# First cross-attention: quantised rows as whole numbers in bf16 with the scales applied to the products, and the first loads in another order

## The chip, the cores and the metric

The kernel runs on one core of a Trainium2 chip. The metric is the time of one execution on the device, in microseconds (us), taken as the median over several executions. The engines are named as in the profile: PE (TensorE, matrix products) with PEld (its weight loads), DVE (VectorE), ACT (ScalarE), POOL (GpSimd) and SP (the engine that issues the DMAs).

## The reference

Six stages run over x, 16 sequences of 32 tokens of 256 features (512 rows): cross-attention, differential attention, an fp8 feed-forward, a second cross-attention, latent attention and a second fp8 feed-forward. The change touches the first. It is preceded by a layer norm of x and followed by the residual sum, and attends to a context of 512 tokens of 256 features for each sequence, with 16 heads of 16 features:

```
s    = max(|row|) / 127                          # one scale per row
qdq(a) = clip(round(a / s), -127, 127) * s
q    = qdq(y) @ qdq(wq).T + bq                   # y = layernorm(x)
k, v = ctx @ wk.T + bk, ctx @ wv.T + bv
o    = softmax(q k.T / 4) v
x    = x + qdq(o) @ qdq(wp).T + bp
```

qdq takes one scale per token for an activation and one per output channel for a weight. Since both scales are constant along the summed features, they can be taken out of the product: (whole numbers of y) @ (whole numbers of wq).T, times the scale of the token, times the scale of the channel.

## The kernel before

The program is written out for each engine in its own order; engines meet at semaphores. The first cross-attention is `xattn` with L0 true, and has two parts.

**The opening** runs up to the first scores. SP issues the loads in one order: x, the key weights, the value weights, the context of batch 0, the key bias, the identity matrix, then wq, wp, the biases and the head mask (`load_rest`), then further contexts (`load_later`). PE first waits for the identity (in `build`), then for three loads of weights and bias (`s_kv_in`) and for the context. It computes keys and values in "units", four to a batch: units 0 and 1 of a batch are the two halves of the keys (L355), units 2 and 3 the values (L361). A unit fills one of two PSUM banks, which ACT (later DVE too) empties into SBUF (L585, L587); a bank must be emptied before the unit after next. ACT takes units 0 to 15 here. Between units, PE turns wq (L509), turns the normed rows of x (L152), forms the queries (L517) and turns wp. DVE prepares these operands: `norm_stats`, then `qdq_rows` on wq, on y and on wp, with copies of what PE turned (L864, L873). ACT and DVE each finish one half of the queries (L690, L870), and POOL spreads them by head (`separate`).

**The batch loop** (`batch_rows_pe`, `batch_rows_act`, `batch_rows_dve`) runs over 16 batches. PE computes four scores (L375), turns four sets of probabilities (`turn`, L400), multiplies them with the values (`values`, L422), and works three or four units ahead for later batches. DVE takes the maxima (L717) and copies half of the turned probabilities (L722); ACT takes the exponentials (L605) and copies the other half (L617). Groups 2 and 3 of a batch are turned and multiplied in the next batch.

Four batches make one tile of 128 output rows. In batches 6, 10 and 14 the loop also finishes a tile: in the batch before, DVE normalises, adds the bias and runs `qdq_rows` on it (`rows_ready`); PE turns it (`turn_out`, L449), ACT copies it (`copy_out_cols`, L634), PE multiplies it with wp (`out_rows`, L458) and DVE adds the product to x (`residual`, L770). The fourth tile is done after the loop. From batch 6 to batch 13, DVE ends each batch with a centring of attention weights for the next stage (L960 to L965).

Of the kernel before, what the change touches and what calls it, by code (L numbers as in the profile page):

```python
# [14 lines left out]
P = 128  # L15
# [164 lines left out]
def qdq_rows(nc, ch, rows, n, q):  # L180
# [8 lines left out]
    for i in range(n):  # L189
        ch.mark(nc.vector.tensor_scalar(rows[:, i, :], rows[:, i, :], -127.0, q.s[:, i:i + 1], ALU.max, ALU.mult))  # L190
    ch.join()


def xattn(nc, e, take, sem, L0, d):
# [3 lines left out]
    s_w, s_kv_in = sem(f"{nm}_weights"), sem(f"{nm}_wkv_in")  # L198
    ctx_in = [sem(f"{nm}_ctx_in{i}") for i in range(CB)]
# [28 lines left out]
    wqT, wpT = (take([P, NC, D]), take([P, NC, D])) if L0 else (wq, wp)  # L228
# [4 lines left out]
    orow, orT = take([P, NT, D]), take([P, NC, P])  # L233
    rc = take([P, 4, H])
    oc = take([P, G, P])
    if L0:
        q = Named(m=take([P, NT]), s=take([P, NT]), r=take([P, NT]))
# [12 lines left out]
    U, S, T, O = (B[0], B[1]), (B[2], B[3], B[4], B[5]), (B[4], B[5]), (B[6], B[7])  # L250
    TURNB, OUTB, YB = O[1], O[0], O[1] if L0 else O[0]
# [89 lines left out]
    def unit_pe(pe, u):  # L341
# [6 lines left out]
        if i == 0:  # L348
            if b == 0:
                pe.wait_ge(s_kv_in, 48)  # L350
            pe.wait_ge(ctx_in[b % CB], 16 * (b // CB + 1))
# [5 lines left out]
        else:  # L357
            for kk in range(2):
# [80 lines left out]
    def turn_out(pe, t):  # L439
# [8 lines left out]
        for c in range(NC):  # L448
            last = nc.tensor.transpose(OUTB[:, c * P:(c + 1) * P], orow[:, t, c * P:(c + 1) * P], e.ident)  # L449
# [55 lines left out]
    def turn_weight(pe, i):  # L505
        pe.wait_ge(s_wq, i + 1)
        for c in range(NC):
            for o in range(NC):
                last = nc.tensor.transpose(B[2 + i][:, c * D + o * P:c * D + (o + 1) * P],  # L509
                                           (wq, wp)[i][:, o, c * P:(c + 1) * P], e.ident)  # L510
        last.then_inc(s_wT, 1)

    def queries(pe):
        pe.wait_ge(e.s_yT_out, f.all)
        for c2 in range(NC):
            for c in range(NC):
                last = nc.tensor.matmul(B[4 + c2], wqT[:, c, c2 * P:(c2 + 1) * P], e.yT[:, c, :],  # L517
# [3 lines left out]
    def pe(pe):  # L521
        if L0:
            for u in range(8):
                unit_pe(pe, u)
            turn_weight(pe, 0)
            for u in range(8, 12):
                unit_pe(pe, u)
            for k in range(2):
                norm_turn(nc, pe, e, f, k, O[k])
            pe.wait_ge(s_wT_out, 1)  # L530
# [4 lines left out]
            pe.wait_ge(s_wT_out, 2)  # L535
# [107 lines left out]
    def batch_rows_act(act, b):  # L643

        copy_out_cols(act, tile_at(b, OUT))
        if b:
            copy_pT_act(act, b - 1, 2)
        exp_rows(act, b, 0), exp_rows(act, b, 1)
# [27 lines left out]
    def act(act):  # L676
        act.wait_ge(s_kv_in, 48)
        if L0:
            for u in range(12):
                unit_act(act, u)  # L680
            for k in range(2):
                norm_cols(nc, act, e, f, k, O[k], e.yT)
# [50 lines left out]
    def rows_ready(v, t):  # L733
# [22 lines left out]
        if L0:  # L756
            e.ch.link(nc.vector.tensor_tensor(orow[:, t, :], orow[:, t, :], bv, ALU.add))
            qdq_rows(nc, e.ch, orow[:, t:t + 1, :], 1, q)
# [4 lines left out]
    def residual(v, t):  # L763
# [74 lines left out]
    def before_dve(v):  # L838
# [8 lines left out]
        nc.vector.tensor_scalar(bs, bq, DH ** -0.5, None, ALU.mult).then_inc(s_small, 1)  # L847

    def dve(v, done):
        if L0:  # L850
# [5 lines left out]
            qdq_rows(nc, e.ch, wq, NC, q)  # L856
            v.sem_inc(s_wq, 1)
            for k in range(2):
                norm_rows(nc, v, e, f, k, e.s_norm)
            v.wait_ge(e.s_norm, NT)  # L860
            qdq_rows(nc, e.ch, e.Y, NT, q)
# [3 lines left out]
            qdq_rows(nc, e.ch, wp, NC, q)  # L865
            v.sem_inc(s_wq, 1)
        else:
            before_dve(v)
        v.wait_ge(s_qT, 2)
        nc.vector.tensor_scalar(qT[:, 1, :], B[5], bq[:, 1:2], DH ** -0.5, ALU.add, ALU.mult).then_inc(s_qT_out, 1)  # L870
        if L0:
            v.wait_ge(s_wT, 2)
            nc.vector.tensor_copy(wpT.rearrange("p c n -> p (c n)"), B[3]).then_inc(s_wT_out, 1)  # L873
# [999 lines left out]

def build(nc, d, out, stages=6):
    with ExitStack() as ctx:
# [8 lines left out]
        neghalf = sb("neg_half", [P, 2 * NT])  # L1884
# [10 lines left out]
        s_const, s_x, s_half, s_chain = sem("constants"), sem("x_in"), sem("neg_half_ready"), sem("dve_chain")  # L1895
        done = [sem(f"phase_done{i}") for i in range(stages)]
# [8 lines left out]
        def _(sp):  # L1905
            sp.dma_start(e.X, d.x.rearrange("(t p) d -> p t d", p=P)).then_inc(s_x, 16)
            phases[X0].load_early(sp, 1)
# [49 lines left out]
        def _(pe):  # L1957
            pe.wait_ge(s_const, 16)
# [80 lines left out]
```

## Time and profile before

| | us |
|---|---|
| median of 3 executions | 745.14 |
| lowest and highest | 739.39, 746.81 |
| profiled execution | 744.93 |
| its span, first to last instruction | 743.1 |
| opening: start to first scores | 45.5 |
| batch loop and last tile: first scores to the last tile's residual sum | 192.3 |

The span is what the rows below are placed in; a start is counted from its beginning. "Busy" is time in which an engine has an instruction under way, and an idle time in brackets names what ended it. The product of two fp32 operands appears in the trace as two passes for each matmul of the program, and a turn (transpose) of an fp32 tile as one.

### The profile page before, as it was taken

To read this page: it belongs to the slowest core of one execution; us is meant where nothing else is said; L and a number is where in the kernel's file an instruction comes from. 1 tells how busy PE (TensorE), PEld (TensorE's weight loads), DVE (VectorE), ACT (ScalarE), POOL (GpSimd) and SP (SyncE) were. 2 spreads that over 40 slices of the span, in tenths; PEclk is the share of its full clock that TensorE was granted. 3 is DMA by queue.
4 is the path that set the end of the run, shared out by engine and by line. 5 is a ranking of instruction groups with operands and counts; after the bars stand their busy time and mean duration, and the time that the engine had idled before them with its cause. 6 is when DMAs were issued, how large, how long until landed. Compare 5 with 4: busy or idle time off the path is not lost.

```text
span 743.1 us, 21667 instructions
## 1 busy us (share of the span) xinstructions
PE 672.0 (90%) x9593; PEld 443.3 (60%) x9594; DVE 424.0 (57%) x979; ACT 278.1 (37%) x503; POOL 76.3 (10%) x138
## 2 busy tenths in 40 slices
PE   4999999999997999999988999999989978899744
PEld 2656566666654677777765566776657754366512
DVE  4324446567475655555533945547757844465477
ACT  1334434344442333333335625444434443121123
POOL 1020000001001011111112412010101001000000
PEclk9999999999999999999999999999999999999967
DMA  5242101114101701110004301111850000000000
GB/s 187 86 147 46 47 30 30 51 38 146 56 2 39 248 30 32 34 36 17 2 1 151 134 28 59 59 31 50 225 169 3 4 2 0 3 4 4 3 1 29
DMA packets 39357, 42.02 MB, mean 57 GB/s; under 512 B 13216, under 2 KB 29856, under 8 KB 39008
## 3 DMA queue, kind: packets, MB, share of 16 engines
q1 hardware_dynamic: 39264, 40.63, 17.6%
q8 instruction: 76, 1.25, 0.7%
q14 instruction: 17, 0.14, 0.1%
HBM read 40.10 MB, written 0.52 MB: 55 GB/s over the span
## 4 chain that ended last, share of the span: by engine, by line
PE 76%; DVE 15%; issue 3%; ACT 3%; POOL 1%; DMA 1%; SPq 0%; DVEq 0%; ACTq 0%; POOLq 0%
PE psum L355 14%; PE psum L361 13%; PE psum L1023 6%; PE psum L422 4%; PE psum L375 4%; PE psum L400 4%; PE psum L389 4%; PE psum L1070 4%; PE psum L1029 3%; PE psum L1678 2%; PE psum L1054 2%; PE psum L1697 2%; DVE arena L1347 1%; PE psum L1043 1%; PE psum L1654 1%
## 5 line engine op out<-in xcount | busy, mean ns | idle before, releaser
L355 PE MATMUL psum<-arena 128*128 128x512 f32 x256 | 125.1, 616 | 11.6 <-DMA ident<-in_ident 9.2
L361 PE MATMUL psum<-arena 128*128 128x256 f32 x512 | 124.4, 389 | 0.4 <-ACT arena L585 0.4
L361 PEld LDWEIGHTS psum<-arena 128*128 128x128 f32 x512 | 94.6, 192 | 24.0 <-issue 9.4
L355 PEld LDWEIGHTS psum<-arena 128*128 128x128 f32 x256 | 45.8, 194 | 57.3 <-issue 42.3
L611 ACT ACTIVATE arena<-arena 128x512 f32<-128x512 f32 x64 | 48.6, 806 | 77.8 <-DVE arena L730 77.8
L422 PEld LDWEIGHTS psum<-arena 128*17 128x17 f32 x4096 | 38.9, 96 | 32.0 <-issue 26.0
L730 DVE TENSOR_SCALAR arena<-psum 128x512 f32<-128x512 f32 x64 | 41.2, 685 | 28.5 <-PE psum L389 27.0
L605 ACT ACTIVATE arena<-psum,arena 128x512 f32<-128x512 f32 x64 | 42.5, 688 | 37.9 <-DVE arena L717 37.8
L717 DVE TENSOR_REDUCE arena<-psum 128x1 f32<-128x512 f32 x64 | 42.4, 685 | 22.7 <-PE psum L375 22.6
L1023 PE MATMUL psum<-y_cols,arena 128*128 128x512 f32 x112 | 52.2, 599 | 0.0
L422 PE MATMUL psum<-arena 128*17 128x32 f32 x4096 | 45.0, 195 | 7.5 <-ACT arena L611 3.4
L303 POOL TENSOR_TENSOR arena<-arena,head_mask 128x128 f32<-128x128 f32 x64 | 24.9, 413 | 217.8 <-PE psum L375 123.3
L1118 ACT ACTIVATE arena<-psum 128x512 f32<-128x512 f32 x48 | 28.2, 597 | 49.8 <-PE psum L1023 31.8
L389 PE MATMUL psum<-arena 64*128 64x128 f32 x512 | 38.1, 288 | 2.4 <-POOL arena L303 1.7
L585 ACT ACTIVATE arena<-psum,arena 128x512 f32<-128x512 f32 x41 | 27.9, 683 | 32.0 <-PE psum L355 31.9
L389 PEld LDWEIGHTS psum<-arena 64*128 64x128 f32 x512 | 31.8, 190 | 12.4 <-issue 8.0
L722 DVE COPY arena<-psum 128x512 f32<-128x512 f32 x32 | 22.1, 690 | 27.5 <-PE psum L400 27.0
L587 ACT ACTIVATE arena<-psum 128x512 f32<-128x512 f32 x41 | 24.3, 594 | 35.1 <-PE psum L361 35.1
L400 PEld LDWEIGHTS psum<-ident,arena 128*128 128x128 f32 x256 | 28.7, 141 | 14.1 <-issue 12.3
L375 PE MATMUL psum<-arena 64*128 64x512 f32 x128 | 36.1, 641 | 0.0
L400 PE MATMUL psum<-ident,arena 128*128 128x128 f32 x256 | 34.1, 276 | 0.8 <-ACT arena L605 0.8
L617 ACT ACTIVATE arena<-psum 128x512 f32<-128x512 f32 x32 | 19.1, 597 | 39.3 <-PE psum L400 39.0
(229 smaller groups left out, 979.9 us busy)
## 6 DMA issues: line engine op xcount, KB each, us to landing
arena<-in_ctxT SPq DMA_DIRECT2D x32, 512.0 KB, 3.7
arena<-in_L_attn_Wv SPq DMA_DIRECT2D x1, 2048.0 KB, 8.3
arena<-in_L_attn_Wq SPq DMA_DIRECT2D x8, 256.0 KB, 2.9
arena<-in_L_attn_Wk SPq DMA_DIRECT2D x8, 256.0 KB, 3.3
arena<-in_L_attn_Wo SPq DMA_DIRECT2D x1, 2048.0 KB, 11.5
arena<-in_L_ffn_w_gating SPq DMA_DIRECT2D x1, 2048.0 KB, 7.8
arena<-in_L_attn_wo SPq DMA_DIRECT2D x1, 2048.0 KB, 10.7
arena<-in_wq_upT SPq DMA_DIRECT2D x1, 1536.0 KB, 8.5
```

The lines of the kernel that those rows point to most:

```text
L355: last = nc.tensor.matmul(bank, wkv[:, c, i * P:(i + 1) * P], x[:, c, :], start=(c == 0), stop=(c == NC - 1))
L361: last = nc.tensor.matmul(bank[:, kk * D:(kk + 1) * D], x[:, c, k * P:(k + 1) * P], wkv[:, c, D:2 * D], start=(c == 0), stop=(c == NC - 1))
L375: nc.tensor.matmul(S[r], qbd[b % 2][a, h, :, :].rearrange("p j q -> p (j q)"), kT[home(b)][a, h, :], start=True, stop=True).then_inc(s_sco ...
L389: ins = nc.tensor.matmul(S[2 * kp + r][:, (2 * kk + h) * P:(2 * kk + h + 1) * P], kT[home(b)][a, h, k * P:(k + 1) * P], qbd[b % 2][a, h, : ...
L400: last = nc.tensor.transpose(T[g % 2][:, k * P:(k + 1) * P], pr[g % 2][:, k * P:(k + 1) * P], e.ident)
L422: last = nc.tensor.matmul(O[b % 2][j * SQ:j * SQ + VW, g * SQ:(g + 1) * SQ], va[home(b)][:, k, HG * g + j, :], probs[:, j * SQ:(j + 1) * S ...
L605: nc.scalar.activation(pr[g % 2], S[g % 2], ACT.Exp, bias=nmx[:, g:g + 1]).then_inc(s_exp, 1)
L611: nc.scalar.activation(pTk[b % 2][k], clip[k // 2][:, k % 2, :], ACT.Exp, bias=mb[:, b, k:k + 1], scale=m01[:, b, k:k + 1]).then_inc(s_exp, 1)
L717: nc.vector.tensor_reduce(nmx[:, g:g + 1], S[g % 2], AX.X, ALU.max, negate=True).then_inc(s_mx, 1)
L730: nc.vector.tensor_scalar(dst, S[i].rearrange("p (a n) -> p a n", n=P), 50.0, -50.0, ALU.min, ALU.max)\
L1023: last = nc.tensor.matmul(bank, w[:, c, f], e.yT[:, c, :], start=(c == 0), stop=(c == NC - 1))
L1070: ins = nc.tensor.matmul(ACC[t // 2][:, (t % 2) * D:(t % 2 + 1) * D], oT[h % 2][:, t, :], wo[:, h, :], start=(h == 0 and t % 2 == 0), stop ...
```

## The change

**Whole numbers.** `qdq_rows` becomes `whole_rows`: the last step, which clipped and multiplied each row by its scale, only clips and writes the whole numbers as bf16 (-127 to 127 are exact there). The turned copies (`wqT`, `wpT`, `yT8`, `orT`) are bf16, so the products for the queries and for the output rows have bf16 operands, and the turns multiply by a bf16 identity, which DVE makes (L904 of the changed kernel).

**Scales.** The token scales are needed along the columns. PE spreads them over a bank with four 128x128 products (`token_scales`), DVE copies that bank to SBUF and applies both scales to each half of the queries; ACT adds the bias to both halves. The channel scales of wp go the same way (`channel_scales`, `swp`), and `residual` first applies both scales, then adds to x.

**Loads and start.** The order is now: key weights, context of batch 0, value weights, key bias, x, identity, and the rest as before. The key weights have a semaphore of their own, so units 0 and 1 wait for it and for the context only; the identity is waited for where it is first used. Before its first unit PE runs three matmuls on a constant (`first_busy`), ACT one small activation.

**Order in a tile's batch.** `turn_out` comes after the two turns of the batch before, `out_rows` after its values; ACT's copies are exchanged likewise.

```diff
-def qdq_rows(nc, ch, rows, n, q):
+def whole_rows(nc, ch, rows, n, q, whole):
...
     ch.link(nc.vector.tensor_scalar(rows, rows, ROUND, 127.0, ALU.subtract, ALU.min))
-    for i in range(n):
-        ch.mark(nc.vector.tensor_scalar(rows[:, i, :], rows[:, i, :], -127.0, q.s[:, i:i + 1], ALU.max, ALU.mult))
-    ch.join()
+    ch.link(nc.vector.tensor_scalar(whole, rows, -127.0, None, ALU.max))
...
-        for dst, src in ((wkv[:, :, 0:D], cols(d.wkT)), (wkv[:, :, D:2 * D], cols(d.wvT))):
-            sp.dma_start(dst, src).then_inc(s_kv_in, 16)
+        sp.dma_start(wkv[:, :, 0:D], cols(d.wkT)).then_inc(s_wk, 16)
         load_ctx(sp, 0)
+        sp.dma_start(wkv[:, :, D:2 * D], cols(d.wvT)).then_inc(s_kv_in, 16)
...
-                pe.wait_ge(s_kv_in, 48)
+                pe.wait_ge(s_wk, 16)
...
+            if u == 2:
+                pe.wait_ge(s_kv_in, 32)
...
+        if b == 0 and g == 0:
+            pe.wait_ge(s_wT_out, 3)
...
-            last = nc.tensor.transpose(OUTB[:, c * P:(c + 1) * P], orow[:, t, c * P:(c + 1) * P], e.ident)
+            cols = slice(c * P, (c + 1) * P)
+            if L0:
+                last = nc.tensor.matmul(OUTB[:, cols], whole[:, t, cols], identb, start=True, stop=True)
...
         scores_rows(pe, b, 0)
-        turn_out(pe, tile_at(b, OUT))
         if b:
             turn(pe, b - 1, 2), turn(pe, b - 1, 3)
+        turn_out(pe, tile_at(b, OUT))
         unit_pe(pe, slot(b, 0))
-        out_rows(pe, tile_at(b, TAKE))
         if b:
             values(pe, b - 1, 2), values(pe, b - 1, 3)
+        out_rows(pe, tile_at(b, TAKE))
...
+    def token_scales(pe):
+
+        pe.wait_ge(s_wT_out, 1)
+        for t in range(NT):
+            nc.tensor.matmul(TOKENS[:, t * P:(t + 1) * P], qx.s[:, t:t + 1].to_broadcast([P, P]), e.ident, start=True, stop=True)
+
+    def channel_scales(pe):
+
+        pe.wait_ge(s_wT_out, 2)
+        pe.wait_ge(s_qT_out, 2)
+        for c in range(NC):
+            last = nc.tensor.matmul(CHANNELS[:, c * P:(c + 1) * P], qp.s[:, c:c + 1].to_broadcast([P, P]), e.ident,
+                                    start=True, stop=True)
...
+            for c in range(NC):
+                act.wait_ge(s_small, c + 1)
+                nc.scalar.activation(qT[:, c, :], qT[:, c, :], ACT.Identity, bias=bs[:, c:c + 1]).then_inc(s_qT_out, 1)
...
+            e.ch.link(nc.vector.scalar_tensor_tensor(out=orow[:, t, :], in0=OUTB[:, D:2 * D], scalar=qx.s[:, 0:1], in1=swp,
+                                                     op0=ALU.mult, op1=ALU.mult))
             v.wait_ge(s_xb, t + 1)
-            nc.vector.tensor_tensor(e.X[:, t, :], OUTB[:, D:2 * D], e.X[:, t, :], ALU.add).then_inc(s_res, 1)
+            nc.vector.tensor_tensor(e.X[:, t, :], orow[:, t, :], e.X[:, t, :], ALU.add).then_inc(s_res, 1)
...
+            v.wait_ge(s_qT, 1)
+            e.ch.link(nc.vector.tensor_copy(pr[0], TOKENS))
+            for c in range(NC):
+                v.wait_ge(s_qT, c + 1)
+                nc.vector.scalar_tensor_tensor(out=qT[:, c, :], in0=B[4 + c], scalar=swq[:, c:c + 1], in1=pr[0],
+                                               op0=ALU.mult, op1=ALU.mult).then_inc(s_small, 1)
+            v.wait_ge(s_wT, 2)
+            nc.vector.tensor_copy(wpT.rearrange("p c n -> p (c n)"), B[3]).then_inc(s_wT_out, 1)
+            v.wait_ge(s_wT, 3)
+            nc.vector.tensor_copy(swp, CHANNELS).then_inc(s_wT_out, 1)
...
+def first_busy(nc, e, bank, n):
+
+    for _ in range(n):
+        nc.tensor.matmul(bank, e.neghalf[:, 0:1].to_broadcast([P, P]), e.neghalf[:, 0:1].to_broadcast([P, 512]),
+                         start=True, stop=True)
...
-            sp.dma_start(e.X, d.x.rearrange("(t p) d -> p t d", p=P)).then_inc(s_x, 16)
             phases[X0].load_early(sp, 1)
+            sp.dma_start(e.X, d.x.rearrange("(t p) d -> p t d", p=P)).then_inc(s_x, 16)
...
-            pe.wait_ge(s_const, 16)
+            pe.wait_ge(s_half, 1)
+            first_busy(nc, e, e.B[5], 3)
...
+            act.wait_ge(s_half, 1)
+            nc.scalar.activation(warm, e.neghalf2, ACT.Identity)
```

Three places of PE's order follow. At the start, before (in brackets the semaphores waited for):

```order
L355 MATMUL psum<-arena 128x512 [waits x0_ctx_in0,x0_wkv_in,constants]
L355 MATMUL psum<-arena 128x512 x3
L361 MATMUL psum<-arena 128x256 [waits x0_unit_out0]
L361 MATMUL psum<-arena 128x256 x3
L361 MATMUL psum<-arena 128x256 [waits x0_unit_out1]
L361 MATMUL psum<-arena 128x256 x3
L355 MATMUL psum<-arena 128x512 [waits x0_ctx_in1,x0_unit_out0]
L355 MATMUL psum<-arena 128x512
```

and with the change, where L359 and L367 are the units' lines L355 and L361:

```order
L1934 MATMUL psum<-neg_half 128x512 [waits neg_half_ready]
L1934 MATMUL psum<-neg_half 128x512 x2
L359 MATMUL psum<-arena 128x512 [waits x0_ctx_in0,x0_wk_in]
L359 MATMUL psum<-arena 128x512 x3
L367 MATMUL psum<-arena 128x256 [waits x0_wkv_in,x0_unit_out0]
L367 MATMUL psum<-arena 128x256 x3
L367 MATMUL psum<-arena 128x256 [waits x0_unit_out1]
L367 MATMUL psum<-arena 128x256 x3
L359 MATMUL psum<-arena 128x512 [waits x0_ctx_in1,x0_unit_out0]
```

The identity ("constants") no longer stands ahead of unit 0, three matmuls on the constant do, and the value weights and key bias are waited for at unit 2.

From the turns of the normed rows to the next unit, before:

```order
L152 MATMUL psum<-ident,y_rows 128x128 [waits y_rows]
L152 MATMUL psum<-ident,y_rows 128x128 x3
L152 MATMUL psum<-ident,y_rows 128x128 [waits y_rows]
L152 MATMUL psum<-ident,y_rows 128x128 x3
L517 MATMUL psum<-y_cols,arena 128x512 [waits y_cols_out,x0_wT_out]
L517 MATMUL psum<-y_cols,arena 128x512 x3
L509 MATMUL psum<-ident,arena 128x128 [waits x0_wqdq]
L509 MATMUL psum<-ident,arena 128x128 x3
```

and with the change:

```order
L531 MATMUL psum<-arena 128x128 [waits y_rows]
L531 MATMUL psum<-arena 128x128 x3
L531 MATMUL psum<-arena 128x128 [waits y_rows]
L531 MATMUL psum<-arena 128x128 x3
L538 MATMUL psum<-ident,arena 128x128 [waits x0_wT_out]
L538 MATMUL psum<-ident,arena 128x128 x3
L553 MATMUL psum<-arena 128x512 [waits y_cols_out]
L553 MATMUL psum<-arena 128x512 x3
L521 MATMUL psum<-arena 128x128 [waits x0_wqdq]
L521 MATMUL psum<-arena 128x128 x3
L359 MATMUL psum<-arena 128x512 [waits x0_ctx_in0,x0_unit_out0]
```

L531 are the bf16 turns, L538 the token scales, L553 the queries, L521 the turn of wp. Four 128x128 products have come in ahead of the queries.

In batch 6, before (L375 scores, L449 `turn_out`, L400 turns, L361 a unit, L458 `out_rows`, L422 values):

```order
L375 MATMUL psum<-arena 128x512 x2
L449 MATMUL psum<-ident,arena 128x128 x2
L400 MATMUL psum<-ident,arena 128x128 x8
L361 MATMUL psum<-arena 128x256 x4
L458 MATMUL psum<-arena 128x256 x2
L422 MATMUL psum<-arena 17x32 x32
L355 MATMUL psum<-arena 128x512 x2
```

and with the change (L381, L459, L408, L367, L470, L430 in their place):

```order
L381 MATMUL psum<-arena 128x512 x2
L408 MATMUL psum<-ident,arena 128x128 x8
L459 MATMUL psum<-arena 128x128 x2
L367 MATMUL psum<-arena 128x256 x4
L430 MATMUL psum<-arena 17x32 x32
L470 MATMUL psum<-arena 128x256 x2
L359 MATMUL psum<-arena 128x512 x2
```

`turn_out` has moved behind eight turns, and `out_rows` behind the 32 products of two groups' values.

## Rows read from the trace of the kernel before

**Rows 1.** Page, busy time by engine: us, share, instructions.
```profile
PE 672.0 (90%) x9593; PEld 443.3 (60%) x9594; DVE 424.0 (57%) x979; ACT 278.1 (37%) x503; POOL 76.3 (10%) x138
```

**Rows 2.** Stretches, 10 to 15 us: PE, PEld, DVE, ACT, POOL busy, PEclk, DMA, GB/s.
```profile
10.00:15.00 5.00, 4.60 (x9) 1.76 (x8) 2.95 (x10) 2.20 (x3) 1.38 (x2) 1.00 0.54 194
```

**Rows 3.** Timeline of the DMA issues: start, us, line, transfer.
```profile
1.24 0.49 SPq L268 DMA_DIRECT2D arena<-in_L_wkT  x1
...
2.29 0.47 SPq L263 DMA_DIRECT2D arena<-in_ctxT  x1
2.80 0.47 SPq L270 DMA_DIRECT2D arena<-in_L_xattn_bkv  x1
...
6.94 18.90 SPq L263 DMA_DIRECT2D arena<-in_ctxT  x4
```

**Rows 4.** DMA issues: KB, us to landing; contexts of batches 0 and 1 last.
```profile
arena<-in_L_wkT SPq DMA_DIRECT2D x1, 256.0 KB, 4.4
...
arena<-in_L_xattn_bkv SPq DMA_DIRECT2D x1, 1.0 KB, 6.1
...
arena<-in_ctxT SPq DMA_DIRECT2D x1, 512.0 KB, 6.4
...
arena<-in_ctxT SPq DMA_DIRECT2D x1, 512.0 KB, 5.8
```

**Rows 5.** Chain of waits, 0 to 62 us: start, us, engine, line.
```profile
9.16 3.56 PE psum L355 x4
...
12.79 1.28 ACT L585
...
14.82 3.72 PE psum L361 x16
18.55 3.44 PE psum L355 x8
...
32.80 0.60 ACT arena L587
...
34.52 3.67 PE psum L517 x8
...
45.53 1.06 PE psum L375 x4
```

**Rows 6.** Timeline of VectorE, 0 to 62 us.
```profile
11.73 0.17 DVE L847 TENSOR_SCALAR arena<-arena 128x2 f32<-128x2 f32 x1 [4.11 <-DMA head_mask<-in_headmask]
...
19.83 1.14 DVE L190 TENSOR_SCALAR y_rows<-y_rows,arena 128x256 f32<-128x256 f32 x4
```

**Rows 7.** Timeline of TensorE in the first feed-forward: 8-bit operands.
```profile
401.41 1.89 PE L1287 MATMUL psum<-arena 128*128 128x512 fp8e4 x8 [0.97 <-ACT arena L160]
```

**Rows 8.** Chain of waits in batch 6, then TensorE's waits, 95 to 230 us.
```profile
113.93 0.87 PE psum L400 x8
...
116.53 0.87 PE psum L458 x4
...
PE psum L449 <- DVEq L759: 1.7, 3, 0.6
```

**Rows 9.** Timeline of VectorE in batch 6, of both in 10, of VectorE in 14.
```profile
120.89 0.69 DVE L722 COPY arena<-psum 128x512 f32<-128x512 f32 x1 [3.03 <-PE psum L400]
...
161.63 0.44 PE L449 MATMUL psum<-ident,arena 128*128 128x128 f32 x2 [0.59 <-DVEq L759]
...
164.47 0.68 DVE L722 COPY arena<-psum 128x512 f32<-128x512 f32 x1
...
165.46 0.73 PE L422 MATMUL psum<-arena 128*17 128x32 f32 x64
...
212.04 0.68 DVE L722 COPY arena<-psum 128x512 f32<-128x512 f32 x1
```

**Rows 10.** Chain of waits at the end of the stage.
```profile
236.26 1.15 PE psum L458 x4
237.43 0.43 DVE x_rows L770
```

More of the change, by code:

```diff
@@ L227, in xattn @@
     wq, wp = take([P, NC, D]), take([P, NC, D])
-    wqT, wpT = (take([P, NC, D]), take([P, NC, D])) if L0 else (wq, wp)
+    wqT, wpT = (take([P, NC, D], BF16), take([P, NC, D], BF16)) if L0 else (wq, wp)
     bq, bs = take([P, NC]), take([P, NC])
@@ L232, in xattn @@
     qT = take([P, NC, ROWS])
-    orow, orT = take([P, NT, D]), take([P, NC, P])
+    orow, orT = take([P, NT, D]), take([P, NC, P], BF16 if L0 else F32)
     rc = take([P, 4, H])
@@ L236, in xattn @@
     if L0:
-        q = Named(m=take([P, NT]), s=take([P, NT]), r=take([P, NT]))
+        qx, qq, qp = (Named(m=take([P, NT]), s=take([P, NT]), r=take([P, NT])) for _ in range(3))
+        wq8 = take([P, NC, D], BF16)
+        wp8 = wq.rearrange("p c n -> p (c n)").bitcast(BF16)[:, 0:NC * D].rearrange("p (c n) -> p c n", c=NC)
+        whole, yT8 = take([P, NT, D], BF16), take([P, NC, ROWS], BF16)
+        identb, swq, swp = take([P, P], BF16), take([P, NC]), take([P, D])
         nmx = take([P, HG])
@@ L508, in turn_weight, with turn_tokens @@
             for o in range(NC):
-                last = nc.tensor.transpose(B[2 + i][:, c * D + o * P:c * D + (o + 1) * P],
-                                           (wq, wp)[i][:, o, c * P:(c + 1) * P], e.ident)
+                last = nc.tensor.matmul(B[2 + i][:, c * D + o * P:c * D + (o + 1) * P],
+                                        (wq8, wp8)[i][:, o, c * P:(c + 1) * P], identb, start=True, stop=True)
+        last.then_inc(s_wT, 1)
+    def turn_tokens(pe, k):
+        ts = f.groups[k]
+        pe.wait_ge(e.s_y, f.y + ts[-1] + 1)
+        for c in range(NC):
+            for j, t in enumerate(ts):
+                a = (c * len(ts) + j) * P
+                last = nc.tensor.matmul(O[k][:, a:a + P], whole[:, t, c * P:(c + 1) * P], identb, start=True, stop=True)
+        last.then_inc(e.s_yT, 1)
+    def token_scales(pe):
[8 more added lines that the diff above has]
+                                    start=True, stop=True)
         last.then_inc(s_wT, 1)
@@ L516, in queries @@
             for c in range(NC):
-                last = nc.tensor.matmul(B[4 + c2], wqT[:, c, c2 * P:(c2 + 1) * P], e.yT[:, c, :],
+                last = nc.tensor.matmul(B[4 + c2], wqT[:, c, c2 * P:(c2 + 1) * P], (yT8 if L0 else e.yT)[:, c, :],
                                         start=(c == 0), stop=(c == NC - 1))
@@ L534, in pe @@
                 unit_pe(pe, u)
-            pe.wait_ge(s_wT_out, 2)
+            channel_scales(pe)
         else:
@@ L687, in act @@
                     unit_act(act, u)
-        act.wait_ge(s_qT, 1)
-        act.wait_ge(s_small, 1)
-        nc.scalar.activation(qT[:, 0, :], B[4], ACT.Identity, bias=bs[:, 0:1], scale=DH ** -0.5).then_inc(s_qT_out, 1)
+        if L0:
+            for c in range(NC):
+                act.wait_ge(s_small, c + 1)
+                nc.scalar.activation(qT[:, c, :], qT[:, c, :], ACT.Identity, bias=bs[:, c:c + 1]).then_inc(s_qT_out, 1)
+        else:
+            act.wait_ge(s_qT, 1)
+            act.wait_ge(s_small, 1)
+            nc.scalar.activation(qT[:, 0, :], B[4], ACT.Identity, bias=bs[:, 0:1], scale=DH ** -0.5).then_inc(s_qT_out, 1)
         for u in range(12 if L0 else FIRST - 2, FIRST):
@@ L757, in rows_ready @@
             e.ch.link(nc.vector.tensor_tensor(orow[:, t, :], orow[:, t, :], bv, ALU.add))
-            qdq_rows(nc, e.ch, orow[:, t:t + 1, :], 1, q)
+            whole_rows(nc, e.ch, orow[:, t:t + 1, :], 1, qx, whole[:, t:t + 1, :])
             v.sem_inc(s_or, 1)
@@ L846, in before_dve @@
             e.ch.join()
[L847 removed]
+        if L0:
+            e.ch.link(nc.vector.tensor_scalar(bs, bq, DH ** -0.5, None, ALU.mult))
+        else:
+            nc.vector.tensor_scalar(bs, bq, DH ** -0.5, None, ALU.mult).then_inc(s_small, 1)
     def dve(v, done):
@@ L860, in dve @@
             v.wait_ge(e.s_norm, NT)
-            qdq_rows(nc, e.ch, e.Y, NT, q)
+            whole_rows(nc, e.ch, e.Y, NT, qx, whole)
             v.sem_inc(e.s_y, NT)
@@ L1883, in build @@
         arena = sb("arena", [P, WORDS])
-        neghalf = sb("neg_half", [P, 2 * NT])
+        neghalf, warm = sb("neg_half", [P, 2 * NT]), sb("act_warm", [P, 2 * NT])[:, :]
         e = Named(
```

33 lines of the change are left out of this document (20 added, 13 removed).

## The prediction

> **What bounds the kernel now.** I read the page first: PE is busy 90% of the span, DVE 57%, ACT 37% [rows 1]. Then the chain of waits and the timeline of the first 62 us, where nearly all edits lie, and then the chain in the batches that finish a tile. In the opening the chain is PE almost without a break from 9.16 us to the first scores at 45.53 [rows 5]. Ahead of 9.16 it is a transfer, the identity matrix. Four things on it are not steady PE work. The start is one. The first four passes take 3.56 us where eight later ones take 3.44, so 0.89 each against 0.43: that is the rate of the 1.2 GHz level, and the later ones that of 2.4. PE had done nothing before them. The granted clock of the stretch reads 1.00 [rows 2, 5], so this slow start has to be read from the passes themselves. ACT's table load at 12.79 delays the first emptied bank, so that unit 2 starts at 14.82. And between the last unit and the queries PE waits for ACT: from 32.80 to 34.52. In the batch loop PE is the chain too, except before the turn of a finished tile [rows 8].
>
> **The start.** Today PE waits for the last of five loads. With the change it needs the key weights and the context of batch 0, now the first two issues. Today the first two (x and key weights, 512 + 256 KB) had landed at 1.24 + 4.4 = 5.64 us [rows 3, 4]; the new pair has the same bytes, so 5.6 is the early bound. The context itself took 6.4 us from its issue; from the second slot, 1.24, that is 7.6, the late bound. It then shared the engines with 1,024 KB ahead of it, now with 256, so I take 6.0, near the early one. Gain 9.16 - 6.0 = **3.2** (1.6 to 3.5).
>
> **The warm-up.** Three fp32 matmuls of 512 columns are six passes. They can start at about 0.9, some 0.1 after the first DMA is issued, since they wait only for a constant that POOL writes first. Four at 0.89 and two at 0.43 give 4.4 us, so they end at 5.3, before the context lands; all six at 0.89 would end at 6.2, a delay of 0.2. The first eight real passes then take 3.44 instead of 3.56 + 1.72: **1.8** less. The table load now runs at about 1 us beside the loads, and unit 2 starts when unit 1 ends: **0.4** less (14.82 - 14.44). The key bias must be there when unit 0 ends, at 7.7: it landed 6.1 after its issue [rows 4], which from its new slot at 2.29 gives 8.4, so bank 0 is empty at about 9.1, still before unit 2 is due at 9.4. I cost it at nothing, or 0.5 if it comes as late as before.
>
> The Trainium skill ("TensorE: Matmul & The Clock Gate", Part 1) says that the point at which the array turns fast varies from run to run of the same kernel, so a fixed number of warm-up matmuls need not reach it. No run here can show that yet; it is the second rival.
>
> **What could now come first.** Everything on PE up to the queries moves 5.4 us earlier, and its partners must keep up. The context of batch 1, issued at 6.94 with 5.8 to landing, is there at 12.7; unit 4 is due at 6.0 + 6.9 = 12.9. That is only just hidden (0 to 0.5 if not). x now lands at about 8.7, as the context did, instead of 4.9. DVE's statistics then take 2.7 us and end near 11.4, and DVE was waiting until 11.73 for the head mask anyway [rows 6]: nothing. The whole numbers of y, finished at about 21 [rows 6], are needed at 27: 6 us of cover.
>
> **Queries.** The gap from the last unit to the queries is ACT's, one bank of 0.60 and two copies, and stays at 1.7 us. The bf16 turns and the four 128x128 scale products (some 1.0 us, eight passes of 0.11 to 0.13) lie inside it. The queries were eight passes in 3.67 us. bf16 has no row of this kind in this stage; the nearest is the fp8 product, eight matmuls of 512 columns in 1.89 [rows 7]: one pass a matmul, some 0.21 each when the first one's start-up is taken off, so 0.11 for 256 columns. Four passes instead of eight twice as long: 0.85 against 3.44, **2.6** less. At the other bound, weight loading that stops bf16 from being faster than one fp32 pass, 1.7 instead of 0.85, it is 1.7 less. Both turns of weights become bf16, four passes that took 0.44 each time: **0.4** less together. `channel_scales` adds two products, four passes, ahead of the scores: **0.5** more.
>
> DVE then has a longer chain than before: copy, two scalings, with ACT's two bias adds behind (five operations of 0.6 to 0.7, two overlapping), and ACT cannot empty units 12 and 13 before the second of them. Queries half one done at 29.1, copy to 29.8, scalings to 30.5 and 31.2, ACT done at 32.0, unit 12 emptied at 32.7; unit 14 is due at 33.1. Hidden by units 12 and 13, with 0.4 to spare; without that cover it would cost its excess one to one. The sum to the first scores: 3.2 + 1.8 + 0.4 + 2.6 + 0.4 - 0.5 = **7.9**.
>
> **The batch loop.** Each of three tiles loses 0.65 in `out_rows` (four passes in 0.87, now two of 0.11) and 0.3 in its turn (0.44 with its start-up [rows 9], now inside the stream). The wait before the turn, 1.7 in three, goes because eight turns (0.87) stand ahead of it [rows 8]. That would be 1.5 a tile. But DVE is late next. In batch 10 its centring work comes after the tile's rows, and its copy for group 3 ends at 165.15, when PE reached the values at 165.46 only because the wait and the slower `out_rows` stood before them [rows 9]. With the change PE is free at 161.63 - 0.59 = 161.04 and reaches group 3 after the turns (0.87), the tile's turn (0.12), a unit (1.72) and group 2 (0.33), at 164.1, and stands 1.0 there. So batch 10 gains 0.5. In batch 14 the copy ends at 212.72, PE gets there at 212.3, gain 1.05. Together 1.5 + 0.5 + 1.05 = **3.1** (0 to 4.6). The extra DVE operation in `residual` (0.43) is covered: DVE idles 3.03 ahead of its next copy [rows 9].
>
> **The last tile** is a chain with no cover: `out_rows` (1.15 there) 0.65 and its turn 0.1 shorter, DVE's two operations in place of one 0.43 more [rows 10]: **0.3** less. Its wait for DVE does not go, since the turn hangs on DVE's rows themselves.
>
> **The sum.** 7.9 + 3.1 + 0.3 = 11.3. Later stages are not touched and follow on the stage's end. The profiled execution took 744.93 (span 743.1); 744.93 - 11.3 = 733.6. It lies 0.2 below the median 745.14, so I predict **733.6** as median too. The three executions spread over 7 us without any row that explains it.
>
> **Rivals.**
> 1. *The forecast*, 0.57: 727.5 to 737, from the late bounds (2.5 less gain) and from the larger loop gain with an early context.
> 2. *The warm-up does not carry*, 0.13: the array is slow again or still when the context lands, and four passes cost 1.8 more, with the transfer late by 1.0: 736.5. For it: PE idles between 5.3 and the landing. Against: that is under 1 us, and PE keeps its speed over the 1.7 us gap before the queries. The rule of the Trainium skill given above stands behind it.
> 3. *The loop gives nothing*, 0.15: PE's gain in a tile's batch turns into a wait for DVE or for ACT's exponentials, as batch 10 half shows. 733.6 + 3.1 = 736.7.
> 4. *bf16 operands do not save the passes*, 0.05: the trace would show as many passes as before. Without 2.6 + 0.4 + 3 x 0.75 + 0.75 = 6.0: 739.6.
> 5. *DVE becomes the bound of the tile batches*, 0.10, slower at its end: `out_rows` now comes later, DVE stands at `residual` for it, with the copy of group 1 and two maxima queued behind, and PE needs those for its next turns. DVE today idles 3 us ahead of that copy; if PE waited out a tile's rows (3.2) and the two residual operations (0.9) in each of three batches, 12.3 us, against 8.2 gained outside the loop, it would be 749. It decides from 2.7 us a tile. Against it: PE has a unit of 1.7 and eight turns between.
>
> **Numbers.** Less than 1% either way (7.4 us, about what a measurement of this kernel can tell) counts as the same. Faster by over 1%, below 737.7: nearly all of cases 1 to 3, less what the spread of the runs takes: 0.77. Same: 0.18, from case 4, the mild end of 5 and drift of the runs. Slower: 0.05, the end of 5. The range 727 to 739.5 leaves out most of case 5 and the tails.
>
> **What would show it.** Right: the first unit near 6.0 with all passes at 0.43; no table load between units; the first scores near 37.6; four query passes in about 1; eight turns, then the tile's turn without a wait; a wait for DVE's copy ahead of group 3's values in batches 10 and 14, near 1.0 and 0.4. Wrong: a first unit after 7.6, slow passes in it, a gap before unit 4 or unit 14, or PE waits in the tile batches above 1.5 us.

## The result, and the profile after

| us | before | changed |
|---|---|---|
| median (4 executions each) | 743.77 | 733.80 |
| lowest and highest | 739.39, 746.81 | 730.49, 735.92 |
| profiled execution, and its span | 744.93, 743.1 | 730.49, 728.7 |

The ratio of the times is 0.9864, 95% interval 0.9827 to 0.99: 10 us faster. A second measurement beside the experiments gave 731.36 against 746.45, ratio 0.9819 (0.9787 to 0.985).

PE is busier by share, for nearly the same work in less time; it remains the bound (the columns are those of [rows 1]):

```profile
PE 669.4 (92%) x9600; PEld 440.9 (61%) x9600; DVE 426.7 (59%) x983; ACT 278.2 (38%) x505; POOL 76.1 (10%) x138
```

The first loads, as KB and us to landing, answer to [rows 4]. The last row is the context of batch 0:

```profile
x_rows<-in_x SPq DMA_DIRECT2D x1, 512.0 KB, 5.9
arena<-in_L_wkT SPq DMA_DIRECT2D x1, 256.0 KB, 2.8
...
arena<-in_L_xattn_bkv SPq DMA_DIRECT2D x1, 1.0 KB, 4.6
...
arena<-in_ctxT SPq DMA_DIRECT2D x1, 512.0 KB, 3.8
```

It had landed at 1.24 + 3.8 = 5.04 us, and the key bias at 2.25 + 4.6 = 6.9. PE's timeline at the start of the changed kernel:

```profile
0.89 4.66 PE L1934 MATMUL psum<-neg_half 128*128 128x512 f32 x6 [0.89 <-POOL neg_half L2014]
5.38 3.60 PE L359 MATMUL psum<-arena 128*128 128x512 f32 x8
...
12.82 3.68 PE L359 MATMUL psum<-arena 128*128 128x512 f32 x8 [0.38 <-DMA arena<-in_ctxT]
```

The six passes of the constant (two for each of the three matmuls) took 4.66 us, the first unit followed them directly (no idle time stands behind the row), all eight of its passes ran at the fast rate, and unit 4 waited 0.38 for its context. The chain of waits through the queries answers to [rows 5]:

```profile
27.15 0.60 ACT arena L624
...
28.78 1.04 PE psum L553 x4
29.82 0.23 PE psum L521 x4
...
37.00 0.44 PE psum L545 x4
37.44 1.06 PE psum L381 x4
```

The gap from the last unit to the queries is 28.78 - 27.15 = 1.63 (1.72 before). The queries take 1.04 instead of 3.67, the turn of wp 0.23, the channel scales 0.44, and the first scores stand at 37.44 instead of 45.53: **8.1 us** earlier.

In the loop, the chain in batch 6, then PE's timeline in batch 10 and the sum of one kind of wait, answer to [rows 8, 9]:

```profile
104.80 1.02 PE psum L408 x8
105.82 0.11 PE psum L459 x2
...
107.71 0.66 PE psum L430 x50
108.38 0.33 PE psum L470 x2
...
155.58 0.43 PE L430 MATMUL psum<-arena 128*17 128x32 f32 x32 [0.83 <-DVE arena L764]
...
PE psum L430 <- DVE arena L764: 1.3, 3, 0.8
```

The tile's turn costs 0.11 behind the eight turns and waits for nothing; `out_rows` costs 0.33 with its start-up. In its place PE now waits for DVE's copy of group 3: 0.83 in batch 10 and 0.18 in batch 14 (the rest of the 1.3 is in the last batch and was there before).

The end of the last tile answers to [rows 10]:

```profile
224.88 0.41 PE psum L470 x2
...
225.31 0.50 DVE arena L811
225.83 0.44 DVE x_rows L814
```

The tile is multiplied in 0.41 instead of 1.15, and DVE applies the scales (L811) in 0.50 before it adds.

From the first scores to the last tile's sum it is now 226.27 - 37.44 = 188.8 instead of 192.3: **3.5 us** less. The stage therefore ends 11.6 earlier, and the rest of the span went from 505.3 to 502.4 although nothing in it was changed. The last section comes back to that.

### The profile page after: what moved, and what is told of

It is laid out like the page before. It is cut to its first block, busy times and chain, and to the rows that moved or that the text cites. A ratio compares the mean times of both kernels' runs of the same rounds, so it can differ in the third digit from the quotient of the medians.

```text
span 728.7 us, 21690 instructions
## 1 busy us (share of the span) xinstructions
PE 669.4 (92%) x9600; PEld 440.9 (61%) x9600; DVE 426.7 (59%) x983; ACT 278.2 (38%) x505; POOL 76.1 (10%) x138
## 4 chain that ended last, share of the span: by engine, by line
PE 77%; DVE 15%; issue 3%; ACT 2%; POOL 1%; SPq 1%; DMA 1%; DVEq 0%; POOLq 0%; ACTq 0%
PE psum L359 13%; PE psum L367 13%; PE psum L1080 7%; PE psum L430 5%; PE psum L381 4%; PE psum L395 4%; PE psum L408 4%; PE psum L1127 4%; PE psum L1086 4%; PE psum L1735 2%; PE psum L1111 2%; PE psum L1754 2%; DVE arena L1404 1%; PE psum L1100 1%; PE psum L1711 1%
## 5 line engine op out<-in xcount | busy, mean ns | idle before, releaser
L359 PE MATMUL psum<-arena 128*128 128x512 f32 x256 | 122.5, 605 | 2.8 <-DVEq L172 2.0
L367 PE MATMUL psum<-arena 128*128 128x256 f32 x512 | 124.3, 388 | 0.0
L367 PEld LDWEIGHTS psum<-arena 128*128 128x128 f32 x512 | 94.6, 192 | 23.3 <-issue 9.7
L359 PEld LDWEIGHTS psum<-arena 128*128 128x128 f32 x256 | 44.7, 189 | 47.7 <-issue 41.9
L430 PEld LDWEIGHTS psum<-arena 128*17 128x17 f32 x4096 | 39.5, 97 | 32.0 <-issue 24.7
L430 PE MATMUL psum<-arena 128*17 128x32 f32 x4096 | 46.1, 197 | 6.2 <-ACT arena L648 3.5
L408 PEld LDWEIGHTS psum<-ident,arena 128*128 128x128 f32 x256 | 28.6, 141 | 16.4 <-issue 14.6
L381 PE MATMUL psum<-arena 64*128 64x512 f32 x128 | 36.1, 641 | 0.0
L408 PE MATMUL psum<-ident,arena 128*128 128x128 f32 x256 | 34.2, 276 | 0.8 <-ACT arena L642 0.8
## 6 DMA issues: line engine op xcount, KB each, us to landing
arena<-in_L_attn_Wo SPq DMA_DIRECT2D x1, 2048.0 KB, 11.7
```

The costliest lines, as they stand in the source:

```text
L359: last = nc.tensor.matmul(bank, wkv[:, c, i * P:(i + 1) * P], x[:, c, :], start=(c == 0), stop=(c == NC - 1))
L367: last = nc.tensor.matmul(bank[:, kk * D:(kk + 1) * D], x[:, c, k * P:(k + 1) * P], wkv[:, c, D:2 * D], start=(c == 0), stop=(c == NC - 1))
L381: nc.tensor.matmul(S[r], qbd[b % 2][a, h, :, :].rearrange("p j q -> p (j q)"), kT[home(b)][a, h, :], start=True, stop=True).then_inc(s_sco ...
L408: last = nc.tensor.transpose(T[g % 2][:, k * P:(k + 1) * P], pr[g % 2][:, k * P:(k + 1) * P], e.ident)
L430: last = nc.tensor.matmul(O[b % 2][j * SQ:j * SQ + VW, g * SQ:(g + 1) * SQ], va[home(b)][:, k, HG * g + j, :], probs[:, j * SQ:(j + 1) * S ...
```

## The experiments

"Opening" is the start of the first scores by PE's timeline (37.37 in the changed kernel, 45.46 before), "loop" the time from there to the end of the last tile's sum (188.9 and 192.4), "rest" what is left of the span. These three are read from one profiled execution of each kernel. "(one)" is the time of a single execution. The rows e1 to e4, e5 to e8 and f1 to f4 are three groups on different chips, so a time is best compared within its group: beside them the kernel before took 744.9, 747.2 (one) and 746.5.

| kernel | first unit | opening | loop | rest | time, us |
|---|---|---|---|---|---|
| before | 9.16 | 45.46 | 192.4 | 505.3 | 743.8 |
| changed | 5.38 | 37.37 | 188.9 | 502.4 | 733.8 |
| e1, start only | 6.17 | 40.18 | 192.9 | 501.1 | 737.0 |
| e2, numbers only | 9.81 | 43.90 | 189.0 | 506.7 | 739.3 |
| e3, no matmuls ahead | 5.31 | 39.41 | 189.2 | 509.7 | 740.0 (one) |
| e4, old order | 6.02 | 37.39 | 189.6 | 502.8 | 731.6 (one) |
| e5, two matmuls ahead | 5.29 | 36.97 | 190.0 | 504.7 | 733.5 (one) |
| e6, context 1 early | 6.17 | 38.00 | 188.9 | 504.2 | 732.9 (one) |
| e7, two more copies | 6.17 | 39.08 | 188.9 | 503.6 | 733.3 (one) |
| e8, centring moved | 6.17 | 37.70 | 190.2 | 503.1 | 732.8 (one) |
| f1, changed again | 5.40 | 37.16 | 188.9 | 502.9 | 731.4 |
| f2, combined | 5.33 | 36.78 | 188.7 | 506.4 | 731.5 |
| f3, paced loads | 6.13 | 37.51 | 188.9 | 503.9 | 732.0 |
| f4, no activation ahead | 5.17 | 37.83 | 188.9 | 501.5 | 730.1 (one) |

### Two halves of the change: e1 and e2

e1 adds to the kernel before:

```diff
+        sp.dma_start(wkv[:, :, 0:D], cols(d.wkT)).then_inc(s_wk, 16)
         load_ctx(sp, 0)
+        sp.dma_start(wkv[:, :, D:2 * D], cols(d.wvT)).then_inc(s_kv_in, 16)
...
+            first_busy(nc, e, e.B[5], 3)
...
+            nc.scalar.activation(warm, e.neghalf2, ACT.Identity)
```

> The kernel before with the start of the change alone (order of the first loads, separate waits, three matmuls and one activation ahead); numbers, scales and the order of the tile batches as before. Theory (the gains of the parts add up on PE's chain): the opening shrinks by what the changed kernel showed at its start, 9.16 - 5.38 = 3.8, plus 1.8 for the fast passes, plus 0.4 for unit 2, minus 0.4 for the wait ahead of unit 4, so 5.6: first scores at 39.9 us; from there to the last tile's sum 192.3 as before; time 5.6 below before. Rival (the start only shifts PE into a wait for DVE or ACT ahead of the queries, which the new numbers alone remove): a gap over 2 us ahead of the queries, first scores at 42 or later.

e2 takes the same lines back from the changed kernel and keeps the rest.

> The changed kernel with the start of before (old order of loads, all of them waited for, no matmuls and no activation ahead). Theory (parts add): first unit at 9.1 us, first scores at 45.5 - 2.5 = 43.0, then 188.8 us to the last tile's sum as in the changed kernel, so 6.0 below before in all. Rival (bf16 operands bring nothing of their own): first scores at 45 or later, loop 192.

PE's timeline of e1:

```profile
0.89 5.49 PE L1881 MATMUL psum<-neg_half 128*128 128x512 f32 x6 [0.89 <-POOL neg_half L1961]
6.17 3.65 PE L356 MATMUL psum<-arena 128*128 128x512 f32 x8
...
29.25 3.67 PE L520 MATMUL psum<-y_cols,arena 128*128 128x512 f32 x8 [0.88 <-ACT y_cols L160]
...
40.18 1.13 PE L378 MATMUL psum<-arena 64*128 64x512 f32 x4
```

and of e2:

```profile
9.81 6.32 PE L359 MATMUL psum<-arena 128*128 128x512 f32 x8 [9.81 <-DMA ident<-in_ident]
...
35.31 1.04 PE L551 MATMUL psum<-arena 128*128 128x512 bf16 x4 [0.27 <-ACT arena L160]
...
43.90 1.13 PE L379 MATMUL psum<-arena 64*128 64x512 f32 x4
```

e1: ratio 0.9923 (0.9885 to 0.996), 5.7 us; opening 5.3 shorter, no gap ahead of the queries beyond the old 0.88, loop as before but for a stall of 0.28. e2: 0.9927 (0.9902 to 0.9952), 5.4 us. Its opening gained only 1.6, as its loads came 0.65 later and its slow passes lasted longer (6.32 for the first eight, 5.26 before), but from the queries to the scores it took 8.59 instead of 10.94, and its loop 189.0. Both rivals fall, and the halves multiply to 0.985, beside 0.9864 and 0.9819 for the whole: **the parts add**, as far as intervals of 2 to 3 us either way on each half can tell. In the profiles the stage ended 4.8 earlier in e1 and 4.9 in e2, together 9.7 of the 11.6; 1.7 of what is missing are the late loads and the longer slow passes of e2.

### The matmuls and the activation ahead: e3, e5, f4

```diff
-            first_busy(nc, e, e.B[5], 3)
```

> The changed kernel without the three matmuls ahead of the first unit. Theory (they take the slow passes upon themselves, and gate the first unit at 5.38 while the context has landed at 5.04): first unit at 5.1, four slow passes of 0.85 to 0.89, units 0 to 3 end 1.4 later than in the changed kernel; of that 0.4 lies in the wait for the context of batch 1, so first scores at 37.4 + 1.0 to 1.4 = 38.4 to 38.9. Rival (the slow passes of before were not PE's idleness but the busy transfers): fast passes from the start, first scores at 37.4 or a little earlier.

```profile
5.31 6.33 PE L359 MATMUL psum<-arena 128*128 128x512 f32 x8 [5.31 <-DMA arena<-in_ctxT]
```

The first unit started at 5.31, 0.2 after its context had landed (1.24 + 3.9), where 5.1 was expected. With the same order of transfers as in the changed kernel, the first eight passes took 6.33 instead of 3.60: 2.7 lost, where 1.4 was expected. Of that 2.0 reached the scores, which stand at 39.41 and not at 38.4 to 38.9. They are slow because PE had done nothing, and there were more slow ones than the four of before. The rival falls; the direction was as expected, the size missed.

```diff
-            first_busy(nc, e, e.B[5], 3)
+            first_busy(nc, e, e.B[5], 2)
```

> The changed kernel with two matmuls instead of three ahead of the first unit (four passes). Theory: they end near 4.5 us, the first unit starts when the context lands, 5.05 to 5.1, with fast passes, since four slow passes were enough before; the 0.3 gained is lost again ahead of unit 4, which waits for the context of batch 1 until 12.8: first scores at 37.4. Rival (the clock needs the third): slow passes in the first unit, first scores at 37.7 or later.

```profile
0.89 3.58 PE L1934 MATMUL psum<-neg_half 128*128 128x512 f32 x4 [0.89 <-POOL neg_half L2014]
5.29 3.68 PE L359 MATMUL psum<-arena 128*128 128x512 f32 x8 [0.82 <-DMA arena<-in_ctxT]
```

The four passes ended before the context, PE idled 0.82, and the unit was fast all the same. The opening was 36.97, 0.4 shorter (0.2 shorter than in f1); the context of batch 1 was there when unit 4 came at 12.41, so that wait did not eat it here. So the third matmul was not needed here, nor in f2 below, which has two as well. Two profiles do not tell what happens when the passes turn fast late: in e6 and e7 the first pass of the first unit was still slow behind six. The loop was 190.0 because of a stall of 0.97 at 179 that names no cause.

f4 leaves out ACT's activation.

> The changed kernel without ACT's small activation ahead. Theory: the table load of 1.28 us comes when unit 0 is done, bank 0 is emptied 1.3 later, and unit 2 starts 0.4 to 0.6 later than the end of unit 1; part of it is taken by the wait for the context of batch 1 where the first unit starts at 5.4, so first scores 0.1 to 0.6 later than in the changed kernel. Rival (a load of the table would have run in ACT's idle time anyway): unit 2 directly behind unit 1.

```profile
7.21 1.28 ACT L622 ACT_TABLE_LOAD   x1 [7.21 <-PE psum L359]
...
9.25 3.72 PE L367 MATMUL psum<-arena 128*128 128x256 f32 x16 [0.40 <-ACT arena L622]
```

Table load at 7.21, unit 2 held for 0.40, opening 37.83, 0.5 to 0.7 later than the two profiles of the changed kernel: as expected.

### The chain behind the queries: e7

```diff
             e.ch.link(nc.vector.tensor_copy(pr[0], TOKENS))
+            e.ch.link(nc.vector.tensor_copy(pr[0], TOKENS))
+            e.ch.link(nc.vector.tensor_copy(pr[0], TOKENS))
```

> The changed kernel with two more DVE copies of 0.69 in the chain from the queries to the emptying of units 12 and 13 (the bank of token scales copied three times; same result). Theory (the longer DVE and ACT chain is hidden with about 0.4 to 0.5 to spare): 1.45 more in the chain makes unit 14 late by 0.9 to 1.1, first scores at 38.3 to 38.5. Rival (it is hidden much deeper): no change, 37.4; other rival (it is not hidden even now): 1.45 later, 38.9.

```profile
30.25 0.39 PE L521 MATMUL psum<-arena 128*128 128x128 bf16 x4
...
34.99 3.72 PE L367 MATMUL psum<-arena 128*128 128x256 f32 x16 [0.86 <-ACT arena L622]
...
39.08 1.13 PE L381 MATMUL psum<-arena 64*128 64x512 f32 x4
```

Unit 14 waited 0.86. One of the four passes of the queries is missing from this trace, so I count from the turn of wp behind them: 39.08 - 30.25 = 8.83 to the scores, against 37.37 - 29.66 = 7.71 in the changed kernel, 1.1 for 1.45 of chain. The longer chain of the changed kernel is hidden, and by only about 0.4: there ACT had emptied unit 12 at 32.90, and unit 14 started at 33.38.

### The order in the tile batches: e4

```diff
         scores_rows(pe, b, 0)
+        turn_out(pe, tile_at(b, OUT))
         if b:
             turn(pe, b - 1, 2), turn(pe, b - 1, 3)
-        turn_out(pe, tile_at(b, OUT))
         unit_pe(pe, slot(b, 0))
+        out_rows(pe, tile_at(b, TAKE))
         if b:
             values(pe, b - 1, 2), values(pe, b - 1, 3)
-        out_rows(pe, tile_at(b, TAKE))
```

> The changed kernel with the old order in the tile batches (the tile's turn straight after the scores, its product ahead of the values, ACT's copy likewise). Theory (the order only helps where DVE's copy for group 3 is not late anyway): from first scores to last tile's sum 0.9 us more than the changed kernel's 188.8: batch 6 0.7 more, batch 10 the same within 0.2, batch 14 0.3 more; three waits of 0.5 for DVE's rows come back. Rival (the wait that was removed is gained in full): 1.7 to 2.0 us more, 0.6 in each of the three.

PE's waits from 95 to 222 us:

```profile
PE psum L459 <- DVEq L801: 1.6, 3, 0.5
...
PE psum L430 <- DVE arena L764: 0.3, 1, 0.3
```

The wait for DVE's rows is back, 1.6 in three, and the loop is 0.74 longer, not 1.7. The waits for the copy of group 3 in batches 10 and 14 are gone in exchange. The rival falls: the new order removes 1.6 of waiting and is worth 0.7, read from one profile (the loop of the changed kernel came again within 0.1 in f1, f3 and f4).

### Can the new wait be removed: e8, then f2

```diff
-                if after and 6 <= b < 6 + H // 2:
-                    e.phases[A0].centre_dve(v, b - 6)
...
         residual(v, tile_at(b, TAKE))
+        if L0 and after and 7 <= b < 7 + H // 2:
+            e.phases[A0].centre_dve(v, b - 7)
         copy_pT_dve(v, b, 1)
```

> The changed kernel with DVE's centring of the next stage's weights (about 1.6 us a batch) moved from the end of batches 6 to 13 into batches 7 to 14, behind the residual sum and ahead of the copy for group 1, where DVE idles up to 3 us. Theory (in batches 10 and 14 PE waits for DVE's copy of group 3 because the centring stands before it): both waits go, loop shorter by 0.8 to 1.3 us than the changed kernel's 188.8. Rival (the copy is late because of the tile's rows, not of the centring, or the centring makes the copy of group 1 late in its new place): 188.8 or longer.

PE's waits from 95 to 210 us:

```profile
PE psum L381 <- ACT arena L642: 1.6, 2, 1.4
PE psum L430 <- DVE arena L795: 1.4, 3, 1.0
```

The waits for the copy of group 3 went, but the scores now waited 1.6 for ACT's exponentials and the values 0.9 more for DVE's normalising of the tile (L795): loop 1.3 longer. My remedy failed; the rival was right about the new place.

> The changed kernel with the context of batch 1 issued right behind the identity matrix, ahead of wq and the other weights. Theory: the wait of 0.38 ahead of unit 4 goes, first scores at 37.0; wq and the head mask land some 1.5 us later, which DVE's 4 to 6 us of cover ahead of the turns hides. Rival (the late head mask moves DVE onto the path): a wait ahead of the turn of wq or of the normed rows, first scores at 37.4 or later.

(e6 issues the context of batch 1 behind the identity, ahead of `load_rest`, and the others behind `load_rest` as before.) The head mask came at 13.1 instead of 11.7 and nothing waited for what DVE made of it. But the first unit started at 6.17 and its first pass was slow, so that unit 4 came at 13.5 and would not have waited anyway: the first scores stood at 38.0 and not at 37.0, and the gain was not shown.

```diff
-                if after and 6 <= b < 6 + H // 2:
-                    e.phases[A0].centre_dve(v, b - 6)
+                if after and b in (3, 4, 6, 7, 8, 10, 11, 12):
+                    e.phases[A0].centre_dve(v, (3, 4, 6, 7, 8, 10, 11, 12).index(b))
```

> The changed kernel with two matmuls ahead instead of three, the contexts of batches 1 and 2 issued ahead of wq, and DVE's centring taken out of batches 9 and 13, in which it follows the rows of a finished tile (it runs in batches 3, 4, 6, 7, 8, 10, 11, 12). Theory: first unit at 5.3 and first scores at 36.6 to 37.0; the waits for the copy of group 3 in batches 10 and 14 (0.83 and 0.18) go, loop 187.8; in all 1.5 us below the changed kernel, which its interval may not tell from nothing. Rival (as with the centring moved behind the residual sum, another wait takes its place): loop 188.9 or longer.

(The edit moves the context of batch 1 alone ahead of wq, as in e6, not that of batch 2.)

```profile
5.33 3.68 PE L359 MATMUL psum<-arena 128*128 128x512 f32 x8 [0.78 <-DMA arena<-in_ctxT]
...
178.01 1.67 PE L367 MATMUL psum<-arena 128*128 128x256 f32 x7 [0.95 <-issue]
```

Opening 36.78, and no wait for the copy of group 3 in either batch. The loop was 188.7 because of a stall of 0.95 at 178 that names no cause, the like of the one in e5; without it 187.7, as expected. In the time it cannot be told: 731.45 against 731.36 for the changed kernel in the same group.

### The changed kernel again, and the stall: f1, f3

> The changed kernel once more, unaltered, beside the others of this group. Theory (its profiled execution was a good one: warm-up with fast last passes, no stall in the second cross-attention): first unit between 5.4 and 6.2 us, first scores 37.4 to 38.0, loop 188.9 within 0.2, and the part after the last tile's sum anywhere from 502 to 507, by whether PE stalls about 3 us near the end of the second cross-attention while the latent attention's weights arrive. Rival (the profiled execution is typical): 5.38, 37.4, 502.4 again.

f1: first unit 5.40, opening 37.16, loop 188.9, rest 502.9; its five executions lay between 730.83 and 736.74. The opening of the changed kernel's profile came again. But of the nine profiles with three matmuls ahead, six had their first unit at 6.0 to 6.2 (e1, e4, e6, e7, e8, f3) and three at 5.2 to 5.4. An opening near 37.4 came from either, as in e4 with 6.02, because the late ones no longer waited for the context of batch 1.

```diff
-                        phases[M1].load(sp)
+                        phases[M1].load(sp, 0)
+                    if b > 13 and ph(M1):
+                        phases[M1].load(sp, b - 13)
```

Part 0 holds the small loads and wq_up, part 1 wkv_up and the rotary weights, part 2 wo.

> The changed kernel with the large weights of the latent attention no longer issued in one go at batch 13 of the second cross-attention, but a third each at batches 13, 14 and 15. Theory (PE's stall of about 3 us there, marked as issue, comes with transfers that hold all DMA engines for 15 us and more; it occurs in some executions only): the stall is absent, the part after the last tile's sum is 502 to 504, and the median is 1 to 2 us below the changed kernel's. Rival (the stall has nothing to do with these transfers, or follows them to their new place): a stall of 1 to 3 us remains somewhere between batches 13 and 15, median as the changed kernel's.

```profile
526.23 1.16 PE L395 MATMUL psum<-arena 64*128 64x128 f32 x15 [1.06 <-issue]
```

A stall of 1.06 at the first third remained, where all the other profiles have one of 0.3 to 1.3. The one of 3 us was absent, as it is in the changed kernel's two profiles, so its absence here shows nothing. The median did not fall, 731.99 against 731.36 for f1: that is what the rival said. The five executions lay within 0.9 us (731.48 to 732.42), where those of f1 spread over 5.9 and those of f2 over 4.2; whether the pacing did that, five executions each do not tell.

## Why the prediction was right

Forecast 733.6, measured 733.8; gain of the stage 11.3 forecast, 11.6 in the profile. That the times agree within 0.2 is luck: the median of the changed kernel was 731.4 in the other group, and that of the kernel before fell from 745.1 to 743.8 with its fourth execution. The gain of the stage is what can be held against the sum. Point by point:

- **Start**, 3.2: measured 3.8 in the changed kernel's profile and 3.0 where the first unit stood at 6.17. The number held by luck, its mechanism did not. The context landed at 5.0, before my early bound of 5.6: that bound rested on the key weights' 4.4 us in the second slot, and in the first slot they took 2.8. What gated the first unit was the warm-up I had costed as free: 4.66 us when its last passes were fast, which cost only 0.1 (without it, in e3, the unit started at 5.31), and 5.3 to 5.5 when five or all six were slow, which held the unit back by 0.7 to 0.9.
- **Fast passes**, 1.8, **table load**, 0.4: 1.7 (3.60 against 5.26) and 0.4, with f4 for the second. That four slow passes were the price was right for one execution: e2 and e3 had more.
- **Context of batch 1**: "only just hidden" came out as a wait of 0.38, so it took back more than half of the 0.6 that the start gave beyond the forecast.
- **Queries**, 2.6 + 0.4 - 0.5: 2.63, 0.43, 0.44. The fp8 rows were a good price for bf16: 1.04 for four passes with their start-up. The chain on DVE and ACT was hidden with about 0.4 to spare, as forecast (e7).
- **Loop**, 3.1, and **last tile**, 0.3: together 3.5. Taken at the end of each tile batch's values (with `out_rows`), batch 6 gave 1.4 (1.5 forecast), batch 10 0.5 (0.5), batch 14 1.1 (1.05), the last tile 0.5 (0.3). The step that mattered was to follow DVE's order to the next late thing: without the wait for group 3 I would have forecast 1.5 a tile.
- **The residual's extra operation** was covered in the loop. At the end it cost 0.50.

Rival 2 (the array slow again when the context lands) did not occur in the changed kernel, and e5 shows that an idle of 0.82 between warm-up and first unit does not slow it. Its half about the switching point did occur: the same six passes of the constant, begun at 0.89 each time, took 4.44 to 5.49 us in nine profiles of eight kernels. The rule of the Trainium skill that the point varies between runs of the same kernel ("TensorE: Matmul & The Clock Gate", Part 1) agrees with that, though the two profiles of the changed kernel itself gave 4.66 and 4.67. Rivals 3, 4 and 5 fell with the loop's 3.5 and the single passes.

## What to carry to other kernels

Price a removed wait by the next thing that is late on the same chain: here 1.6 us of waiting turned out to be worth 0.7. A start that waits for several loads should wait only for the two that the first product reads, and warm-up work must end before they land, or it becomes the start itself, as it did in six of nine profiles here. When single profiles differ by more than the stages explain, compare the unchanged stages before believing the total.

## What the runs showed of the hardware

**PE stalls that name no cause, during a long burst of transfers.** In the second cross-attention, which the change does not touch, the kernel before has this in PE's timeline:

```profile
547.35 0.60 PE L422 MATMUL psum<-arena 128*17 128x32 f32 x48 [2.85 <-issue]
...
549.60 2.98 PE L355 MATMUL psum<-arena 128*128 128x512 f32 x4
```

and in the stretches around it (PE, PEld, DVE, ACT, POOL busy, granted clock, DMA share, GB/s):

```profile
540.00:543.00 3.00, 3.00 (x27) 2.42 (x26) 2.86 (x6) 0.60 (x1) 0.00 (x0) 1.00 1.10 368
...
546.00:549.00 3.00, 1.65 (x60) 1.60 (x62) 0.00 (x0) 0.69 (x3) 0.00 (x0) 0.87 0.72 261
549.00:552.00 3.00, 3.00 (x12) 1.50 (x9) 1.29 (x2) 0.99 (x2) 0.00 (x0) 0.56 0.01 3
```

PE stood 2.85 us between two groups of the same loop, "issue", while the DMA engines had been full (share 0.98 and more in every stretch of 3 us from 528 to 546) with the weights of the latent attention and two contexts. After it the granted clock read 0.87 and 0.56, and a row of four passes of L355 took 2.98 us instead of 1.99. The changed kernel had nothing of the kind in the same place:

```profile
532.29 1.59 PE L430 MATMUL psum<-arena 128*17 128x32 f32 x128
533.81 1.16 PE L395 MATMUL psum<-arena 64*128 64x128 f32 x16
534.90 1.99 PE L359 MATMUL psum<-arena 128*128 128x512 f32 x4
```

Of 14 profiled executions five had the stall at 2.6 to 3.2 us (before, e2, e3, e5, f2), with a rest of 504.7 to 509.7; the other nine had at most 1.3 there and a rest of 501.1 to 504.2. The clock fell behind it in four of the five, not in e5. The stall accounts for the 2.9 us by which the two profiles differ beyond the stage, and so for most of the step from 10, by which the medians differ, to the 14.4 by which the profiles do. It may also be behind the spread of the single times, but only the profiled executions can be looked into.

The burst alone does not make the stall. The changed kernel, without it, had the engines just as full (share 1.04 and more in every stretch of 3 us from 517 to 535), and so had e1, at 0.99 and more from 523 to 544. What holds PE up no run shows.

**How soon a load lands hangs on its place in the queue.** The key weights took 2.8 us from the first slot and 4.4 from the second, behind x. The context of batch 0 took 3.8 from the second slot, behind 256 KB, and 6.4 to 7.1 from the fourth, behind 1,024 KB (before, e2).
